# A two-layer sequence model on one core: twin LSTM banks, new places for the decays, softplus and layer 0, and attention squares on ScalarE and TensorE

## The reference, cut to what matters

```python
# block 1: a selective state space model, 256 channels, 16 states
delta = softplus(dt_raw * W_dt[:, 0] + b_dt)
h = exp(delta * A) * h + delta * b_t * u_t          # over 1024 tokens
y = sum_s(h * c_t) + D * x_d;  y = y * silu(z)
# block 2: 16 experts of 64, top 2, and a shared expert of 352
# block 3: an LSTM of 20 units gives every token mu and sigma
g = x_t @ W_ih.T + h @ W_hh.T + b                   # 4 gates
c = sigmoid(f) * c + sigmoid(i) * tanh(gg);  h = sigmoid(o) * tanh(c)
w = exp(-(i / (j + 1) - mu) ** 2 / (2 * sigma ** 2))  for i <= j, else 0
context = (w / sqrt(sum(w * w))) @ x                # over all tokens up to j
# block 4: four layers, each 4 experts of 512 with Gelu, top 2
```

## Time and profile before

| | us |
|---|---|
| three executions, median (lowest to highest) | 3310.76 (3310.53 to 3321.73) |
| the profiled execution | 3320.64 |
| its span, first to last instruction | 3318.9 |
| granted clock of TensorE, mean over the span | 0.777 |
| TensorE, VectorE, ScalarE, POOL busy | 2623.6, 1966.8, 1439.5, 1037.4 |

### The profile page before, as it was taken

The page is one execution under the profiler, slowest core; times in us unless marked ns, Lnnn a source line. Parts: engine busy times, 40 slices in busy tenths (PEclk is TensorE's granted clock), DMA queues, the critical chain, the costliest instruction groups (busy, mean ns, idle before and its releaser), DMA issues.

```text
span 3318.9 us, 30820 instructions
## 1 busy us (share of the span) xinstructions
PE 2623.6 (79%) x7208; PEld 1313.7 (40%) x7208; DVE 1966.8 (59%) x6585; ACT 1439.5 (43%) x4660; POOL 1037.4 (31%) x913
## 2 busy tenths in 40 slices
PE   3767784479886888688887888688878997699598
PEld 1222542244433343344334343443434444444344
DVE  4766785367755667467656676557656454444422
ACT  3232433245543555445544554445543444344333
POOL 4744454025431344144332354135332000200200
PEclk7587556568985899679886898679876997598688
DMA  3131331013220322123220232113210211011021
GB/s 109 61 87 46 105 109 51 0 45 92 76 70 23 89 80 73 33 63 86 82 59 22 86 87 63 30 53 91 68 55 22 67 55 42 17 60 61 19 77 54
DMA packets 111779, 204.71 MB, mean 62 GB/s; under 512 B 14801, under 2 KB 24424, under 8 KB 111596
## 3 DMA queue, kind: packets, MB, share of 16 engines
q1 hardware_dynamic: 111596, 202.75, 20.7%
HBM read 195.36 MB, written 7.34 MB: 61 GB/s over the span
## 4 chain that ended last, share of the span: by engine, by line
PE 41%; DVE 28%; ACT 15%; issue 7%; POOL 1%; DVEq 0%; POOLq 0%; ACTq 0%
PE p_hid L647 8%; DVE state L1192 7%; PE p_gates L900 7%; PE p_misc L657 4%; ACT cell_t L914 4%; DVE cell L930 3%; DVE add_c L927 3%; DVE weighed L1201 2%; PE p_acc L657 2%; PE p_misc L355 2%; DVE p_gates L924 2%; PE p_hid L583 2%; DVE hist L933 2%; DVE terms L809 2%; ACT cand L911 1%
## 5 line engine op out<-in xcount | busy, mean ns | idle before, releaser
L900 PEld LDWEIGHTS p_gates<-hist,w_hh 22*128 22x128 f32 x2048 | 383.0, 231 | 1236.7 <-DVE hist L933 1073.3
L900 PE MATMUL p_gates<-hist,w_hh 22*128 22x4 f32 x2048 | 468.8, 297 | 485.8 <-DVE hist L933 469.8
L647 PE MATMUL p_hid<-xhat,w 128*128 128x512 f32 x1024 | 612.8, 684 | 1.1 <-ACT hid L705 0.7
L924 DVE SCALAR_TENSOR_TENSOR p_gates<-p_gates,cell 20x4 f32<-20x4 f32 x1024 | 170.7, 167 | 636.4 <-ACT p_gates L910 618.0
L914 ACT ACTIVATE cell_t<-cell 20x4 f32<-20x4 f32 x1024 | 207.7, 203 | 728.4 <-DVE cell L930 728.4
L705 ACT ACTIVATE hid<-p_hid,b1f 128x512 f32<-128x512 f32 x512 | 351.6, 687 | 291.7 <-PE p_misc L657 200.5
L1130 POOL TENSOR_TENSOR drive<-du,rows 128x512 f32<-128x512 f32 x256 | 445.3, 1740 | 67.8 <-DVE state L1192 50.5
L389 POOL TENSOR_TENSOR n_rstd<-n_var,minus_half 128x4 f32<-128x4 f32 x56 | 61.9, 1105 | 1269.5 <-DVE n_var L377 1269.5
L1192 DVE TENSOR_TENSOR_SCAN state<-decay,drive 128x512 f32<-128x512 f32 x256 | 404.9, 1582 | 28.2 <-POOL drive L1134 16.9
L1149 POOL TENSOR_TENSOR y<-y,weighed 128x512 f32<-128x512 f32 x192 | 242.4, 1262 | 573.4 <-DVE weighed L1201 573.0
L933 DVE SCALAR_TENSOR_TENSOR hist<-p_gates,cell_t 20x4 f32<-20x4 f32 x1024 | 162.7, 159 | 275.5 <-ACT cell_t L914 275.5
(11 more groups left out here) (208 smaller groups left out, 3329.0 us busy)
## 6 DMA issues: line engine op xcount, KB each, us to landing
rows<-rows_dram SPq DMA_DIRECT2D x128, 512.0 KB, 5.1
w<-w_dram SPq DMA_DIRECT2D x128, 256.0 KB, 2.7
w<-in_w2T SPq DMA_DIRECT2D x128, 256.0 KB, 2.7
comb_b<-comb_dram SPq DMA_DIRECT2D x64, 512.0 KB, 4.6
rows<-comb_dram SPq DMA_DIRECT2D x128, 128.0 KB, 2.9
w<-in_w1T SPq DMA_DIRECT2D x16, 256.0 KB, 2.6
w_dram<-w SPq DMA_DIRECT2D x16, 256.0 KB, 2.0
out_xT<-result SPq DMA_DIRECT2D x8, 256.0 KB, 2.6
```

The lines of the kernel that those rows point to most:

```text
L647: nc.tensor.matmul(p_hid[:, v % 2, :], w1[:, v // FB, (v % FB) * P:(v % FB + 1) * P], xhat[:, :], start=True, stop=True).then_inc(g_h, 1)
L900: nc.tensor.matmul(p_gates[:, :, t:t + 1], w_hh[:, :], hist[:, :, t:t + 1], start=False, stop=False, skip_group_check=True).then_inc(gates ...
L924: nc.vector.scalar_tensor_tensor(out=gate(32), in0=gate(32), scalar=1.0, in1=cell[32:32 + PE_, :], op0=ALU.add, op1=ALU.mult).then_inc(kee ...
```

## The change

1. Two PSUM banks, `p_turn`, take the places of `p_gates` and `p_acc0` and swap by chunk: gates of chunk i in bank i % 2, sums of `layer0` for chunk q in bank q % 2. The input matmul of a chunk is issued at the end of `layer0`, and `hist` has two halves; `hprev` and both copies go.
2. The attention's squares are made by ScalarE, exp(-2*z*z) for all blocks but the last, the square of the masked tile for the last, and each is summed by TensorE into `p_misc1`. POOL has no part in it. TensorE's rounds begin two steps earlier.
3. Decays: two in steps 0, 1, 2 of a layer, one in 3 and 22. ScalarE asks for Exp's table behind the last Gelu of layers 0 to 2 while there are scans, and behind the softplus' Ln.
4. The softplus of a unit begins in the tail, behind `pre`, and goes on in the next period; its instructions are spread over 13 steps instead of 9. `layer0` begins at step 4 of a period instead of 0.
5. In the last layer x3 is added to the layer's input at v == 4, and not to the first sum at v == 11.

```diff
-    p_gates = psum("p_gates", [P, B, CH])
-    p_acc0 = psum("p_acc0", [P, CT])
+    p_turn = [psum(f"p_turn{k}", [P, CT]) for k in range(2)]
+    gate_bank = lambda i: p_turn[i % 2].rearrange("p (b t) -> p b t", b=B)
+    acc0_bank = lambda q: p_turn[q % 2]
...
 def layer0_pe(q):            # its end
         mm.then_inc(xt_done, 1)
+        yield
+        if q == 0:
+            pe.wait_ge(loaded, 11 * 16)
+        pe.wait_ge(n0.src_ready, q + 1)
+        nc.tensor.matmul(gate_bank(q), w_ih[:, :], x2[:, :].rearrange("p (b t) -> p b t", b=B),
+                         start=True, stop=False, skip_group_check=True).then_inc(in_gates, 1)
...
 def layer1_pe(q):
-        pe.wait_ge(h_saved, q + 1)
+        pe.wait_ge(h_done, (q + 1) * CH)
...
-        for _ in range(6):
+        for _ in range(4):
             yield
...
+        def squares(i):
+            pe.wait_ge(sq_done, past(q) + i + 1)
+            for j in range(B):
+                mm = nc.tensor.matmul(p_misc1[:, j:j + 1], tile(at_s[:, i % 2, :], j), ones[:, :],
+                                      start=(i == 0 and j == 0), stop=False, skip_group_check=True)
+            mm.then_inc(ss_part, 1)
...
+            if i < q:
+                squares(i)
+            yield
+        squares(q)
...
 def layer1_act(q):
             nc.scalar.activation(at_w[:, i % 2, :], at_q[:, :], ACT.Exp, scale=-1.0).then_inc(w_done, 1)
+            if i < q:
+                if i >= 2:
+                    act.wait_ge(ss_part, past(q) + i - 1)
+                nc.scalar.activation(at_s[:, i % 2, :], at_q[:, :], ACT.Exp, scale=-2.0).then_inc(sq_done, 1)
...
+        act.wait_ge(wm_done, q + 1)
+        if q >= 2:
+            act.wait_ge(ss_part, past(q) + q - 1)
+        nc.scalar.activation(at_s[:, q % 2, :], at_m[:, 0, :], ACT.Square).then_inc(sq_done, 1)
...
+                    if v == UN - 1 and l < L - 1 and q + 3 < NCH:
+                        act.preload_act_table(ACT.Exp)
...
 def layer1_dve(q):
-                if l == L - 1 and v == 2 * FB + 3:
-                    dve.wait_ge(g_summed, n * E1 + 1)
-                    nc.vector.tensor_tensor(part[:, :], part[:, :], x3[:, :], ALU.add).then_inc(g_x, 1)
+                if l == L - 1 and v == 4:
+                    nc.vector.tensor_tensor(part[:, :], src, x3[:, :], ALU.add).then_inc(g_x, 1)
...
 def layer1_pool(q):
-            nc.gpsimd.tensor_tensor(square if i else total, weights, weights, ALU.mult).then_inc(sq_done, 1)
-            pool.wait_ge(sq_done, past(q) + i + 1)
-            if i:
-                nc.gpsimd.tensor_tensor(total, total, square, ALU.add).then_inc(ws_done, 1)
...
 def lstm_pe(i):
-        nc.tensor.matmul(p_gates[:, :, :], w_ih[:, :], x2[:, :].rearrange("p (b t) -> p b t", b=B),
-                         start=True, stop=False, skip_group_check=True).then_inc(in_gates, 1)
+            before = hist[:, i % 2, :, t - 1:t] if t else hist[:, 1 - i % 2, :, CH - 1:CH]
...
 def lstm_dve(i):
-        nc.vector.tensor_copy(hprev[0:PE_, :, :], hist[0:PE_, :, 1:CH + 1]).then_inc(h_saved, 1)
-        nc.vector.tensor_copy(hist[0:PE_, :, 0:1], hist[0:PE_, :, CH:CH + 1]).then_inc(h_carried, 1)
...
 def period(i, of, soft):
-            if layer0 and not (heavy and slot < CH):
+            if layer0 and not (heavy and slot < CH) and slot >= (L0_AT if layer1 else 0):   # L0_AT = 4
                 next(layer0, None)
+            if u + 1 < NCH and done["pre"] > PRE:
+                advance(soft_next, "soft", SOFT)
             if u < NCH:
-                if done["soft"] <= SOFT:
-                    if layer1 is None or slot >= 6:
-                        advance(soft, "soft", SOFT)
+                if soft[1] <= SOFT:
+                    next(soft[0], None)
+                    soft[1] += 1
...
-                if layer1 and att - 2 <= slot < tail - 2:
-                    for _ in range({21: 1, 22: 1, 0: 1, 1: 2, 2: 1, 3: 1, 4: 1}.get(o, 0)):
+                if layer1 and att - 1 <= slot < tail - 2:
+                    for _ in range({22: 1, 0: 2, 1: 2, 2: 2, 3: 1}.get(o, 0)):
                         next(burst, None)
```

More of the change, by code:

```diff
@@ L599, in layer1_pe @@
             mm.then_inc(ctx_part, 1)
+            if i < q:
+                squares(i)
             yield
[L601 to L605, removed]
+        squares(q)
+        yield
+        for _ in range(5):
             yield
@@ L818, in add @@
                 done = e == E1 - 1
-                nc.vector.tensor_tensor(xl[:, (l + 1) % 2, :] if done else part[:, :], part[:, :] if e else src,
+                first = part[:, :] if l == L - 1 else src
+                if e == 0 and l == L - 1:
+                    dve.wait_ge(g_x, q + 1)
+                nc.vector.tensor_tensor(xl[:, (l + 1) % 2, :] if done else part[:, :], part[:, :] if e else first,
                                         terms[:, e % 2, :], ALU.add).then_inc(n1.src_ready if done else g_summed, 1)
@@ L1065, in mamba_soft_act @@
             nc.scalar.activation(t_abs[:, j, :], t_abs[:, j, :], ACT.Ln, bias=1.0).then_inc(soft_ln, 1)
-        yield
-        for _ in range(4):
+        act.preload_act_table(ACT.Exp)
+        for _ in range(6):
             yield
@@ L1070, in mamba_soft_act @@
         nc.scalar.activation(kc[:, :, :, :], kc[:, :, :, :], ACT.Exp).then_inc(kc_exp, 1)
-        yield
-        yield
+        for _ in range(3):
+            yield
     def mamba_soft_dve(u):
@@ L1091, in mamba_soft_dve @@
             yield
-        yield
-        yield
-        yield
+        for _ in range(3):
+            yield
     def mamba_soft_pool(u):
         pool = nc.gpsimd
-        for _ in range(3):
+        for _ in range(5):
             yield
@@ L1400, in body, with period @@
     PREP = NB * TAPS + 2
-    def period(i, of):
+    L0_AT = 4
+    def period(i, of, soft):
         lstm = of.get("lstm")
@@ L1409, in period @@
         early = False
-        get = lambda what, n, *a: of[what](u, *a) if what in of else nothing(n)
-        soft = scan = leave = None
+        get = lambda what, n, u, *a: of[what](u, *a) if what in of else nothing(n)
+        scan = leave = pre = soft_next = None
         if u < NCH:
-            soft, scan, leave = get("soft", SOFT), get("scan", SCAN, early), get("leave", LEAVE, early)
-        pre = (of["pre"](u + 1) if "pre" in of else nothing(PRE)) if u + 1 < NCH else None
+            scan, leave = get("scan", SCAN, u, early), get("leave", LEAVE, u, early)
+        if u + 1 < NCH:
+            pre, soft_next = get("pre", PRE, u + 1), get("soft", SOFT, u + 1)
         burst = of["decays"](u) if u < NCH and "decays" in of else nothing(NS)
-        ends = att_slots(i - 1) + L * LAYER + 5 if layer1 else 0
-        done = dict(soft=0, scan=0, leave=0, fold=0, pre=0)
+        att = att_slots(i - 1) if layer1 else 0
+        ends = att + L * LAYER + 5 if layer1 else 0
+        done = dict(scan=0, leave=0, fold=0, pre=0, soft=0)
         fold_slots = 3 * L * E1 + 12 + 1
         slot = 0
-        more = True
         def advance(g, what, n):
@@ L1464, in period @@
                 advance(pre, "pre", PRE)
-            if slot == CH - 1:
-                next(lstm, None)
             slot += 1
@@ L1470, in period @@
                 pass
+        return [soft_next, done["soft"]]
     def opening(of):
@@ L1504, in whole @@
             of["start"]()
+        soft = [of["soft"](2) if "soft" in of else nothing(SOFT), 0]
         for i in range(NCH + 1):
-            period(i, of)
+            soft = period(i, of, soft)
     with nc.Block() as block:
```

94 lines of the change are left out of this document (39 added, 55 removed).

## The result

| | before | changed |
|---|---|---|
| median, us | 3316.24 | 3191.30 |
| lowest to highest (4 runs each) | 3310.53 to 3322.55 | 3184.90 to 3200.67 |
| ratio, 95% interval | | 0.9625 [0.9587, 0.9663] |
| profiled execution / its span, us | 3320.64 / 3318.9 | 3185.66 / 3183.9 |

What follows compares the result with a forecast made beforehand. No engine is full: the chain runs round engines, and queued work beyond ScalarE's 0.86 us of slack lengthens each LSTM step. Terms -87 - 18 - 6 + 0 = -111 us from 3310.8 gave 3200 us, range 3160 to 3260.

Steps and rivals of the forecast that it cites:

- decays and tables: In the layers: 40 ScalarE table loads go and the clock mostly stays high in steps 6 to 9; -87 us.
- boundary: Between periods: copies of h and the input gates' matmuls leave the chain, 2.6 us at each of 7 boundaries; -18 us.
- add of x3: In the last layer: the add no longer stands before a scan, -1.2 us in periods 1 to 5; -6 us.
- head: late layer 0: Head of a period: layer 0 starting 4 steps later frees about 3 us and costs 2.5 in the tail; about 0.
- head: softplus: Head and tail: the softplus keeps all its instructions, spread one to a step over the tail; about 0 in sum.
- head: squares: Attention's rounds: squares moved from POOL to ScalarE and TensorE, costs and savings about equal; about 0.
- 15 of 20 layers at the high clock: Layers with decays: 15 gain 5.0 us each at 2.4 GHz in steps 6 to 9, the other 5 gain 2.4.
- Rival 2: Layers' steps 6 to 9 stay at the low clock, all 20 gaining 2.4 us; -72, 3239 us, chance 0.22.
- the set-off: Attention's rounds in the heads: higher clock, lost wait and lost POOL traffic give back about the +20 us of longer first rounds.
- Rival 4: Heads: TensorE bounds the attention at 1.2 GHz with layer 0 in the same steps; +25, 3225 us, chance 0.07.
- heads that grow: Sign of rival 4: heads of periods 2 to 7 not within 5 us of now plus the boundary's 2.6, but growing.
- Rivals 5 and 6: 5: layers' paired table loads stay, 3287 us, chance 0.03. 6: attention's squares serialise ScalarE and TensorE, slower, chance 0.04.

Runs made afterwards that it cites:

- e4: The changed kernel with layer 0 started in the first step of a period again; 3192.03 us, ratio 0.9611 to the kernel before.
- e1: The kernel before with only the new places of the decays and the Exp table asked for behind a layer's last Gelu; 3232.15 us, ratio 0.9724.
- e2: The kernel before, decays unmoved, with six added matmuls in steps 5 and 6 of each layer with decays, filling TensorE's idle time; 3282.95 us, ratio 0.9878.
- e6: The changed kernel with the attention's squares given back to GpSimd and TensorE's rounds beginning two steps later again; 3175.21 us, ratio 0.9569 to the kernel before.
- e11: The changed kernel with x3 added in the middle of the last layer again, behind the first expert's sum; 3211.81 us, ratio 0.9665 to the kernel before.
- e9: The changed kernel with the attention's squares written and summed in bf16, four matmuls a round instead of eight; 3137.60 us, ratio 0.9449 to the kernel before.
- e12: The changed kernel with the squares of both the attention and the layer norms written and summed in bf16; 3113.41 us, ratio 0.9370 to the kernel before.
- e8: The changed kernel with f32 squares streamed past a stationary column of ones into one row, turned at the end; 3196.60 us, ratio 0.9639 to the kernel before.

## Why the prediction was right

| term | forecast | measured |
|---|---|---|
| decays and tables | -87 | -88 alone, +98 undone |
| boundary | -18 | -21 alone |
| add of x3 | -6 | -14 by the times, -11.5 by the steps |
| head: late layer 0 | about 0 | 0 (e4: 3.5 the other way) |
| head: softplus | about 0 | 0 |
| head: squares | about 0 | +16 |
| sum | -111 | -107 to -117 by the parts, -125 in one |

The parts are a mixture: some were measured alone and some by taking them out.

**The tables.** Steps 5 (2.1 by the means, 1.9 forecast) and 6 to 9 (3.7; 1.0 + 2.6 forecast) shrank by what the steps of the argument said, and steps 0 to 4 grew by 0.7 where 0.5 was put. The one choice that I had hedged, 15 of 20 layers at the high clock, fits the decays alone (16 of 20 in e1). In the changed kernel all 20 are at 1.00: every one took 1.71 to 2.17, 2.25, 1.93 and 2.34 in its steps 6 to 9, but for one whose step 6 was 3.63. Rival 2 is refuted by e1 and e2 together.

The Trainium skill (ScalarE: Activation LUTs, "What ACT_TABLE_LOAD costs") would have put 55 us on top for the drains of 40 switches. With the switches gone, e1 gained 88, and the sum from the rows without drains was 87: no room for it here either.

**The boundary** was right in size, and in place at six of seven: 2.5 us of the first step (2.2 in period 5), and nothing in period 3, where the softplus took it. **The add of x3** was right in its step (1.67 for 4.09 to 2.42, where 1.2 was taken) and missed a second step: I asked what the add delays at its old place and not what it pushes at the new one.

**The head** is the term that was mis-sized, by 16 us. The cost of a round was about right: 4.4 us of TensorE at 1.2 GHz, and period 7 shows 4.01 and period 8, without the LSTM's 0.52, 3.42. What failed is the set-off "the higher clock, the lost wait and the lost POOL traffic give about as much back". The clock did not rise but fell, 0.61 to 0.50 in the head of period 5. The wait did go, and that was worth nothing: ScalarE waited for TensorE's rounds for 34.4 us before and for 2.6 in the changed kernel, and in e6 it waits 32.9 us again and is faster all the same. The changed kernel, then e6:

```profile
L694 ACT ACTIVATE hid<-xhat 128x512 f32<-128x512 f32 x36 | 22.7, 630 | 4.6 <-PE p_acc L612 2.6
```

```profile
L686 ACT ACTIVATE hid<-xhat 128x512 f32<-128x512 f32 x36 | 22.7, 629 | 38.1 <-PE p_acc L604 32.9 <-POOL xl L865 4.6
```

And period 8, where I counted 2 gained from the end of GpSimd's chain, became 3.7 longer, since sixteen f32 instructions at 1.2 GHz (3.42) are more than GpSimd's two (1.04 + 1.26). Rival 4 named it: TensorE with layer 0 in the same steps makes up to 5.96 us; its price was put at 25 and the squares' part of it is 16. But the sign by which I would have known it, heads that grow, did not show. Rivals 5 and 6 didn't occur: 83 loads, and no round above 6 us.

**Luck in the sum.** By place the forecast was less good than its total. It put about -93 us on the layers, -18 on the heads with the boundary, and little on the tails; the profile shows -119, -53 and +39. The heads of periods 2 and 3 fell by 13.4 and 8.5 us, outside the "within 5 us of now plus the boundary's 2.6". That the larger gains in layers and heads and the loss in the tails left a sum near 111 was not worked out.

**Open.** The parts give 107 to 117, the whole 125, 13 more or less. That is inside the uncertainty. By place they do not add up: in the heads the boundary, layer 0, the softplus and the squares, each measured by itself, make -18, -12, -8 and +22, which is 16 of the 53 us; what brought the rest, two parts together or the clock, no run shows. Of the difference in the sum, some is no effect of the change: the opening's -5.9 also appears in e2 (328.3 us against 333.8), which has the opening of before, and not in e1 (334.6). Single layers with the same instructions differ by up to 4 us between runs (e11's first three layers of a period against the changed kernel's).

## What to carry to other kernels

Look for the table switch that stands between two users of the other table: its price is its own time, plus what the engine waiting for it does to its clock while it idles. Before a reduction is moved to TensorE, count the stationary loads, not the columns, and give them a 16-bit type if the values allow. A head, a tail or a layer that shortens proves nothing by itself: the heads here gained 53 us and the tails lost 39.

## What the runs showed of the hardware

- **Stationary operands of 128 x 128 with one streamed column.** From the start of a group of four products to the start of the instruction behind it: in f32 (eight instructions, two for each product) 1.57 to 1.80 us at 1.2 GHz and 0.81 to 0.92 at 2.4, so 0.2 and 0.11 an instruction; in bf16 (four, one for each) 0.13 to 0.22 and mostly 0.10 to 0.12, so 0.03 to 0.06 and 0.03. An f32 group at 2.4 GHz in the changed kernel, for the two of e9 above:

```profile
1508.14 1.05 PE L346 MATMUL p_acc<-mean_w,esig 128*128 128x1 f32 x8
1509.06 0.68 PE L464 MATMUL p_gate<-mid_x,w_gate 128*128 128x512 f32 x1
```

  By line, over the whole run, changed kernel and then e12, for the norms' sums:

```profile
L346 PE MATMUL p_acc<-mean_w,esig 128*128 128x1 f32 x320 | 49.8, 277 | 5.9 <-ACT esig L361 3.8
```

```profile
L350 PE MATMUL p_acc<-mean_h,esig 128*128 128x1 bf16 x160 | 10.1, 167 | 6.0 <-ACT esig L365 3.8
```

  The Trainium skill (TensorE: Matmul & The Clock Gate, "Weight-path perf modes — Fast Weight Load (FWL) and DoubleRow") says that 128 weights of a type other than FP32 are loaded in a fast mode, about twice as fast. The direction agrees; by the starts above an instruction here is 4 times shorter at 2.4 GHz and 4 to 6 times at 1.2.
- **A TensorE that is busy all the time can stay at 1.2 GHz.** Two windows of 14.5 us in period 8's rounds, the changed kernel and e8, where the same squares stream as 512 columns:

```profile
2995.50:3010.00 14.50, 14.50 (x69) 14.50 (x70) 1.44 (x2) 6.30 (x10) 0.00 (x0) 0.50 0.01 1
```

```profile
3020.00:3034.50 14.50, 13.23 (x68) 7.17 (x68) 3.03 (x5) 8.00 (x13) 0.23 (x1) 1.00 0.00 1
```

  The first is 100% busy by the profile, with small instructions, at 1.2 GHz; the second is 91% busy at 2.4. e8's earlier stretch of the same rounds was at 0.53; it rose within them, and the changed kernel's never did.
- **VectorE's scan and GpSimd's product slow each other by order of start**: 1.87 and 1.27 us when the product starts first, 1.40 and 2.18 when the scan does. In the changed kernel the 65 scans that no GpSimd instruction overlaps take 1.22 at the median.
